# Mixture-of-experts phases of a four-layer block: shared down products in float32r, rest terms and sums on GpSimd, turned rows stored by ScalarE

## The reference, cut to what matters

```
x = x + ffn(layernorm(x))                       # before and after attention
logits = einsum('th,eh->te', x, gate_w)         # E = 8 experts, top K = 2
probs = softmax(logits); topk_w, topk_i = top_k(probs, 2); topk_w /= sum(topk_w)
g = einsum('th,ehi->eti', x, w_gate); u = einsum('th,ehi->eti', x, w_up)      # I = 352
eo = einsum('eti,eih->eth', silu(g) * u, w_down)
out = einsum('te,eth->th', combine, eo)
so = silu(x @ sw_gate) * (x @ sw_up) @ sw_down  # the shared expert, all tokens
out = out + sigmoid(x @ shared_gate_w) * so
```

## Time and profile before

| | us |
|---|---|
| median of the runs | 1923.58 |
| profiled execution, own time | 1933.64 |
| its span | 1931.9 |
| TensorE busy | 1852.8 (96%) |
| VectorE busy | 1354.6 (70%) |
| ScalarE busy | 1173.1 (61%) |
| GpSimd busy | 432.4 (22%) |
| first MoE phase, about | 212 to 635 |
| second MoE phase, about | 1510 to 1932 |
| one shared step with a piece of one-hots (steps 11 to 18 on TensorE) | 4.35 |
| VectorE: `hidden_rest` (L658), `source_rest` (L483), mean | 0.56, 0.42 |
| VectorE: the three operations of a one-hot piece (L615, L617, L620) | 0.75, 1.22, 0.75 |
| ScalarE: cast of 704 weight columns (L338) | 0.79 |

### The profile page before, as it was taken

How to read it: one execution, slowest core, us unless ns; L and a number is a source line. 1 busy time by engine, 2 the same in 40 slices (tenths; PEclk the granted TensorE clock), 3 DMA queues, 4 the chain that set the end, 5 groups by cost and what they waited for, 6 DMA issues and landing times. The chain is left out here.

```text
span 1931.9 us, 51788 instructions
## 1 busy us (share of the span) xinstructions
PE 1852.8 (96%) x19838; PEld 1431.7 (74%) x19838; DVE 1354.6 (70%) x2718; ACT 1173.1 (61%) x2355; POOL 432.4 (22%) x509
## 2 busy tenths in 40 slices
PE   7999899999999887999999999999999999999997
PEld 5788789999999644555555555565546789999997
DVE  7566678444436777899999999999944877444445
ACT  4222544444445543898899989989895644445443
POOL 4122001555542322000000000000000002555541
PEclk9999999999999999999999999999999999999999
DMA  7000211222226565321212111111005311222228
GB/s 306 1 1 1 79 45 35 72 77 78 76 68 200 140 171 144 80 52 47 52 47 47 41 42 42 41 42 42 3 3 200 103 36 35 77 75 78 76 68 267
DMA packets 86539, 149.13 MB, mean 77 GB/s; under 512 B 35620, under 2 KB 69284, under 8 KB 80612
## 3 DMA queue, kind: packets, MB, share of 16 engines
q1 hardware_dynamic: 68428, 103.24, 17.8%
q0 software_dynamic: 17856, 42.60, 8.0%
q10 hardware_dynamic: 24, 0.02, 0.0%
HBM read 96.68 MB, written 48.76 MB: 75 GB/s over the span
## 5 line engine op out<-in xcount | busy, mean ns | idle before, releaser
L2212 ACT ACTIVATE att_scores_pt<-att_scores_psE 128x512 f32<-128x512 f32 x1024 | 598.0, 597 | 69.0 <-PE att_scores_psE L1716 26.9
L1731 DVE TENSOR_REDUCE att_mx<-att_scores_psS 128x1 f32<-128x1024 f32 x472 | 577.9, 1224 | 50.1 <-PE att_scores_psS L1716 18.9
L1716 PE MATMUL att_scores_psE<-att_qs,att_ks 99*32 99x512 bf16 x4096 | 437.3, 382 | 4.0 <-DVE att_scores_psO L2242 3.2
L2314 PE MATMUL att_scores_psO<-att_scores_pt,att_va 128*17 128x256 f32 x4096 | 330.4, 379 | 2.9 <-ACT att_scores_osb L2217 1.3
L1716 PE MATMUL att_scores_psS<-att_ks,att_qs 96*32 96x512 bf16 x3776 | 308.4, 380 | 0.1
L1716 PEld LDWEIGHTS att_scores_psE<-att_qs,att_ks 99*32 99x32 bf16 x4096 | 136.0, 95 | 104.0 <-ACT att_scores_pt L2212 8.5
L658 DVE TENSOR_TENSOR moe_hidT_rest<-moe_ps,moe_hidT_high 128x384 fp32r<-128x384 f32 x142 | 79.1, 557 | 184.5 <-ACT moe_hidT_high L377 167.6
L2314 PEld LDWEIGHTS att_scores_psO<-att_scores_pt,att_va 128*17 128x17 f32 x4096 | 131.5, 98 | 103.3 <-issue 13.2
L865 PE MATMUL moe_ps<-W_rest,moe_srcT_high 128*128 (+2 forms) x824 | 200.6, 325 | 0.0
L283 POOL DMA_INDIRECT expert_rows<-work,moe_slots_i x142 | 140.0, 986 | 218.7 <-ACT work L399 101.3
L1716 PEld LDWEIGHTS att_scores_psS<-att_ks,att_qs 96*32 96x32 bf16 x3776 | 126.0, 97 | 78.1 <-issue 1.6
(11 more groups left out here) (325 smaller groups left out, 3154.0 us busy)
## 6 DMA issues: line engine op xcount, KB each, us to landing
W_gate_up<-in_gate_up_dram SPq DMA_DIRECT2D x2, 6346.0 KB, 22.3
work<-expert_rows SPq DMA_DIRECT2D x12, 1024.0 KB, 7.6
query_key_parts<-att_qkv_parts SPq DMA_DIRECT2D x64, 192.0 KB, 3.0
normalised_rows<-work SPq DMA_DIRECT2D x64, 128.0 KB, 1.9
att_qs<-query_key_parts SPq DMA_DIRECT2D x16, 384.0 KB, 4.4
att_ks<-query_key_parts SPq DMA_DIRECT2D x16, 384.0 KB, 4.5
W_down<-in_down_a_dram SPq DMA_DIRECT2D x2, 2304.0 KB, 28.0
work<-normalised_rows SPq DMA_DIRECT2D x36, 128.0 KB, 2.1
```

The costliest lines, as they stand in the source:

```text
L1716: last = nc.tensor.matmul(out[j:j + 32, :], stationary[:, j:j + 32], moving, start=True, stop=True, tile_position=(0, j), skip_group_check ...
L1731: return nc.vector.tensor_reduce(a.mx[g % 2][:, v:v + 1], bank[:, :, :].rearrange("p h k -> p (h k)"), AX.X, ALU.max)
L2212: nc.scalar.activation(pt[s % 2][:, r, :], psE[use % E_BANKS][:, :], ACT.Exp, scale=HD ** -0.5).then_inc(p_ready, 1)
L2314: last = nc.tensor.matmul(psO[32 * r:32 * r + VC, cols], va[g][:, kt, r * VC:(r + 1) * VC], pt[s % 2][:, r, cols], start=(kt == 0 and part ...
```

## The change

- **Down products.** In shared and late steps `down` makes the 9 float32r matmuls that routed steps make. A new `shared_down_high` holds the high part of the shared down weights (ScalarE, at the end of look step 0), its rest is made by GpSimd. ScalarE copies the hidden rows into the single `hidT_high` in every step, and VectorE makes `hidT_rest` in every step (`hidden_rest`).
- **Turned rows.** The look steps have the transposed rows of tiles 4 to 31 in `extra_T` already. ScalarE's queue stores them to a new DRAM tensor `turned_rows` (`store_turned`, 28 DMAs per phase); SyncE loads those of tiles 4 to 21 back already turned. For these 18 tiles TensorE's two transposes go, ScalarE casts the loaded tile, and GpSimd makes its rest (`loaded_rest`). `extra_T` has 7 buffers in place of 2.
- **GpSimd** makes the 16 rests of the routed gate and up weights, half of the 12 rests of the routed down weights, the 18 rests of loaded rows, one multiplication of each of the eight one-hot pieces (`tile_marks`), and the first of `combine`'s two sums (`pair`). VectorE loses these.

The core of the diff (waits, GpSimd's new functions and their order, ScalarE's stores, the callers on VectorE and TensorE):

```diff
 
+        turned = lambda n: not LOOK <= n < NA
+        turns = lambda n: n + 1 if n < LOOK else n + 1 - (NA - LOOK)
+        rest_made = lambda n: (srcT_split, turns(n)) if turned(n) else (loaded_split, n - LOOK + 1)
...
-        SPLIT_REST = {FOUND - 1: range(0, 1), FOUND: range(1, 3), FOUND + 1: range(3, 6), FOUND + 2: range(6, 9),
-                      FOUND + 3: range(9, 12)}
+        SPLIT_REST = {FOUND + 2: range(4, 7), FOUND + 3: range(7, 10)}
+        SPLIT_REST_POOL = {TABLES + 1: range(0, 1), TABLES + 2: range(1, 2), TABLES + 3: range(2, 3), TABLES + 4: range(3, 4), NA: range(10, 12)}
...
+            def load_turned(n):
+                x = n - LOOK
+                sp.wait_ge(T_stored[x % BESIDE], 16 * (x // BESIDE + 1))
+                sp.dma_start(src[ring(n)][:, 0:D], xt_d[:, x, :]).then_inc(early_loaded[ring(n) - 2], 16)
...
-            for n in range(LOOK, NA):
-                x = n - LOOK
-                sp.wait_ge(x_stored[x % BESIDE], 16 * (x // BESIDE + 1))
-                if n >= LOOK + SRC - 2:
-                    sp.wait_ge(T_done, n - (SRC - 2) + 1)
-                sp.dma_start(src[ring(n)][:, 0:D], kept[:, n, 0:D]).then_inc(early_loaded[ring(n) - 2], 16)
+                if n == 2:
+                    for first in range(LOOK, LOOK + SRC - 2):
+                        load_turned(first)
+            for n in range(LOOK + SRC - 2, NA):
+                sp.wait_ge(*rest_made(n - (SRC - 2)))
+                load_turned(n)
...
-            pool.wait_ge(hot_ready, 1)
-            nc.gpsimd.memset(cw[:, :, :], 0.0).then_inc(cw_zero, 1)
...
+            def shared_down_rest():
+                pool.wait_ge(shared_down, 1)
+                nc.gpsimd.tensor_tensor(W["down_rest"][:, :, SHARED, :], W["down"][:, :, SHARED, :], shared_down_high[:, :, :],
+                                        ALU.subtract).then_inc(shared_down_split, 1)
...
+            def loaded_rest(n):
+
+                pool.wait_ge(srcT_ready, n + 1)
+                nc.gpsimd.tensor_tensor(srcT_rest[0].rearrange("p k t -> p (k t)"), buffer(n)[:, 0:D],
+                                        srcT_high[0].rearrange("p k t -> p (k t)"), ALU.subtract).then_inc(loaded_split, 1)
...
+            def tile_marks(i):
+
+                pool.wait_ge(hot_ready, i + 1)
...
+                nc.gpsimd.tensor_tensor(hot_id[i % 2][:, :, 0, :], hot_j[:, :, :],
+                                        tile1[:, i * PIECE:(i + 1) * PIECE, None].to_broadcast([P, PIECE, NBT]), ALU.mult).then_inc(tiles_marked, 1)
...
+            def downs_rest(some):
...
+                    raw, high, rest = down_piece(i)
+                    pool.wait_ge(down_high, i + 1)
+                    nc.gpsimd.tensor_tensor(rest, raw, high, ALU.subtract).then_inc(early_down_rest, 1)
...
+            for i in range(5):
+                weights_rest(i)
+            shared_down_rest()
+            for i in range(5, KD * E):
+                weights_rest(i)
+            for n in range(LOOK, FOUND + 2):
+                loaded_rest(n)
+                i = n - 2 - TABLES
+                if 0 <= i < CH // PIECE:
+                    tile_marks(i)
+                if i == 0:
+                    nc.gpsimd.memset(cw[:, :, :], 0.0).then_inc(cw_zero, 1)
+                if n - 2 in SPLIT_REST_POOL:
+                    downs_rest(SPLIT_REST_POOL[n - 2])
...
-            for j in range(AHEAD):
+            for j in range(2):
                 fetch(j)
+            for n in range(FOUND + 2, NA):
+                loaded_rest(n)
+            for j in range(2, AHEAD):
+                fetch(j)
+            downs_rest(SPLIT_REST_POOL[NA])
...
+            def pair(q):
+
+                at = got[q % GOT]
+                pool.wait_ge(got_loaded[q % GOT], 16 * (q // GOT + 1))
+                nc.gpsimd.tensor_tensor(at[:, :, 0, :], at[:, :, 0, :], at[:, :, 1, :], ALU.add).then_inc(paired, 1)
+
+            for q in range(3):
+                pair(q)
             for g in BY_DMA:
                 pool.wait_ge(added[g], 16)
                 add_rows(g, 1)
+            for q in range(3, len(BY_DVE)):
+                pair(q)
...
-                nc.scalar.copy(extra_T[x % 2][:, :, :].rearrange("p k t -> p (k t)"), psX[x % BESIDE % 2][:, 0:D]).then_inc(x_srcT, 1)
+                if x >= BESIDE:
+                    act.wait_ge(T_stored[x % BESIDE], 16 * (x // BESIDE))
+                nc.scalar.copy(extra_T[x % BESIDE][:, :, :].rearrange("p k t -> p (k t)"), psX[x % BESIDE % 2][:, 0:D]).then_inc(x_srcT, 1)
+
+            def store_turned(x):
+                act.wait_ge(x_srcT, x + 1)
+                nc.scalar.dma_start(xt_d[:, x, :], extra_T[x % BESIDE].rearrange("p k t -> p (k t)")).then_inc(T_stored[x % BESIDE], 16)
...
 
             def source_out(n, u):
 
-                act.wait_ge(T_done, n + 1)
-                nc.scalar.copy(srcT_high[u].rearrange("p k t -> p (k t)"), psT[:, 0:D]).then_inc(srcT_ready, 1)
+                high = srcT_high[u].rearrange("p k t -> p (k t)")
+                if turned(n):
+                    act.wait_ge(T_done, turns(n))
+                    nc.scalar.copy(high, psT[:, 0:D]).then_inc(srcT_ready, 1)
+                    return
+                act.wait_ge(early_loaded[ring(n) - 2], 16 * ((n - LOOK) // (SRC - 2) + 1))
+                act.wait_ge(u_done, n)
+                nc.scalar.copy(high, buffer(n)[:, 0:D]).then_inc(srcT_ready, 1)
+
+            def shared_down_split_high():
+                nc.scalar.copy(shared_down_high[:, :, :], W["down"][:, :, SHARED, :]).then_inc(shared_down, 1)
...
+                if 0 < here <= LOOK:
+                    for i in range(BESIDE - 2, BESIDE):
+                        store_turned((n - 1) * BESIDE + i)
...
                     for i in range(2, BESIDE):
+                        store_turned(n * BESIDE + i - 2)
...
+                    if n == 0:
+                        shared_down_split_high()
...
             def source_rest(n, u):
+                if not turned(n):
+                    return
...
             def choose_second():
+                for u in range(BESIDE):
+                    dve.wait_ge(T_stored[u], 16 * (EX // BESIDE))
...
-                    dve.wait_ge(inv_ready, i)
+                    dve.wait_ge(tiles_marked, i)
...
                 nc.vector.tensor_tensor(hot_p[i % 2][:, :, :], iota_p[:, None, :].to_broadcast([P, PIECE, P]),
-                                        over(pos_p, P), ALU.is_equal)
-                dve.wait_ge(hot_ready, i + 1)
-                nc.vector.tensor_tensor(hot_id[i % 2][:, :, 0, :], hot_j[:, :, :], over(tile1, NBT), ALU.mult).then_inc(inv_ready, 1)
+                                        over(pos_p, P), ALU.is_equal).then_inc(inv_ready, 1)
...
                 at, t = got[q % GOT], BY_DVE[q] * GS
-                dve.wait_ge(got_loaded[q % GOT], 16 * (q // GOT + 1))
-                nc.vector.tensor_tensor(at[:, :, 0, :], at[:, :, 0, :], at[:, :, 1, :], ALU.add)
-                dve.drain()
+                dve.wait_ge(paired, q + 1)
                 dve.wait_ge(d_used, shared_added)
                 nc.vector.tensor_tensor(X[:, t:t + GS, :], X[:, t:t + GS, :], at[:, :, 0, :], ALU.add).then_inc(by_dve, 1)
...
-                if k == "routed":
-                    hidden_rest(n)
+                hidden_rest(n)
...
                 if rows_rest and half == 0:
-                    pe.wait_ge(srcT_split, n + 1)
+                    pe.wait_ge(*rest_made(n))
...
+                if n == 0:
+                    pe.wait_ge(shared_down, 1)
+                    pe.wait_ge(shared_down_split, 1)
+                shared = isinstance(e, int) and e == SHARED
+                for stationary, rests in ((hidT_high, False), (hidT_high, True), (hidT_rest, False)):
+                    if stationary is hidT_rest:
+                        pe.wait_ge(hidT_split, n + 1)
+                    for k in (range(KI - 1, -1, -1) if stationary is hidT_rest else range(KI)):
+                        if rests:
+                            weights = W["down_rest"][:, k, e, :]
+                        else:
+                            weights = shared_down_high[:, k, :] if shared else D_high[k][:, e, :]
+                        last = nc.tensor.matmul(psD[:, 0:D], stationary[:, k, :], weights, start=(stationary is hidT_high and not rests and k == 0),
+                                                stop=(stationary is hidT_rest and k == 0))
...
-                if here + 1 < NS:
+                if here + 1 < NS and turned(here + 1):
```

114 lines of the change are left out of this document (50 added, 64 removed).

## The result

The changed kernel takes 1954.23 us (median of 4 executions, 1951.18 to 1957.67) against 1923.99 us for the kernel before beside it: ratio 1.0161, 95% interval 1.0138 to 1.0183. The forecast was 1931.8.

The account below looks back on a forecast made before the run. TensorE, busy 96% of the span, was taken as the bound. Two phases of 0 - 5.4 + 5.5 = +0.1, plus +7.5 and +0.5 for late steps, gave +8.2: 1931.8 us, own range 1926 to 1938, wider range 1918 to 1943.

Parts of the forecast that it names:

- GpSimd's rests, "cost nothing": Sixteen gate-up rests and one shared down rest on GpSimd, 22 us, beside ScalarE's casts and needed only later: cost nothing.
- The rival with that mechanism: GpSimd and VectorE slow each other in steps 11 to 14: 1939 us with half the 1.8 us loss per step; chance 0.14.
- The line of 1.21 ns a column: GpSimd two-input operations: 1.21 ns a column above 0.42 us, giving 1.66 us for a 1024-column sum.
- The rule weighed in the prediction: Skill's GpSimd rate, about 2.6 cycles an element: 2.25 us for the 1024-column sum, whole sum about 0.6 us higher.
- Down products and transposes: Shared steps: float32r down products save 0.21 us a step, dropped transposes 0.13; shared steps from 9 on at 3.43 us.
- Steps 4 to 21 without the stop: Shared steps 4 to 21: -5.4 us per phase, from -6.1 with less gain in table steps 4 to 8.
- Look steps: Steps 0 to 3: products -0.6, transposes -0.1, add_shared waits -1.1, ScalarE's cast +0.8, 28 stores +1.0; sum 0.
- Tiles 20 and 21: Their rests wait behind slots and two gathers on GpSimd: TensorE stops 4.5 us per phase, clock fall +1.0; together +5.5.
- 323.4: Time in us at which TensorE wants tile 20's rest, after down, hidden transposes and a third of a gate-up.
- the first gather starts at 324.5: GpSimd's first gather, at 324.84 us before, starts 0.35 earlier when VectorE loses source_rest there.
- Late steps: VectorE waits 2.5 us for GpSimd's first sum, 7.5 for the fourth behind an accumulating DMA: +7.5 first phase, +0.5 second.
- Adding to the median: Difference worked out in the profiled execution (1933.64 us), then added to the median of 1923.58 us.

Follow-up runs that it names:

- m1: Short program replacing the kernel: six VectorE forms alone, then beside four GpSimd 704-column sums; six 512-column SBUF sums took 3.70 us alone, 9.58 beside.
- e1: Changed kernel with both sums of every combine on VectorE again, as before the change; ratio 1.0112 to the kernel before.
- e7: Changed kernel with combine sums, rests of tiles 20 and 21, marks and down rests on VectorE, shared down cast one place later; ratio 1.0014 to the kernel before.
- e16: Kernel before with shared down products in float32r alone, hidden_rest on VectorE every step, shared down cast after tile 1's copy, its rest on GpSimd; ratio 1.0015.
- e3: Changed kernel with the rests of loaded tiles 20 and 21 on VectorE instead of GpSimd; ratio 1.0116 to the kernel before.
- e11: Changed kernel with first sums still on GpSimd, but in turn with VectorE's, the first ahead of the accumulating DMAs; late steps 45.9 and 40.7 us.
- e10: Changed kernel keeping only float32r down products and turned rows; weight, row and down rests, marks and sums on VectorE, cast one place later; ratio 1.0019.
- e13: Changed kernel, unchanged, timed and profiled again; ratio 1.0156 to the kernel before.
- e15: Kernel before with each of the 28 look-step rows stored a second time by SyncE, to a place nothing reads; ratio 1.0019.

## Why the prediction was wrong

- **GpSimd's rests, "cost nothing": this step failed.** The text asked when a result is needed, and not what VectorE runs beside GpSimd. The rival with that mechanism had 0.14 and was priced in four steps per phase alone, at 7 us. In its place the runs showed VectorE and GpSimd holding each other (m1) in every stage that got work on GpSimd: VectorE's normalising operations at 811 ns for 413, GpSimd's three operations of a table step at 4.64 us for the 2.9 forecast, a wait of 1.8 us in step 22, and the sum of 5.64 us for 1.22 in the late steps. Taken off GpSimd, the sums give back 12.3 us (e1), and marks and down rests bring steps 12 to 17 from 26.5 to 23.8 us in each phase (e7). The Trainium skill, SBUF — State Buffer, section "Who interferes with whom", says which forms: VectorE's tensor_scalar in its two-port mode, and its instructions with two SBUF inputs against a GpSimd instruction that reads SBUF, while reductions and one PSUM operand are free. By that rule the six forms of m1 come out as measured. The prediction had cited only the short line of the Trainium skill's GPSIMD Engine Reference, "1. Specifications", which speaks of contention.
- **Durations of GpSimd.** The line of 1.21 ns a column gave 1.66 us for 1024 columns; 2.34 measured. The rule weighed in the prediction said 2.25, and was nearly right. The line went through two operations of different kinds, and the time depends on the kind: 704 columns took 1.67 us in m1 and 1.43, alone, as a weight rest in the changed kernel.
- **Down products and transposes.** Forecast 3.43 us for a shared step, 3.34 to 3.36 measured in steps 4 and 5. e16 has 3.56 for 3.78 to 3.80 in step 5, so the products are worth 0.22 to 0.24, where 0.21 was forecast; the transposes 0.2, not 0.13.
- **Steps 4 to 21 without the stop, -5.4 forecast.** Before the stop (steps 4 to 17) -0.4 and -0.1 came. With GpSimd's marks and down rests away e7 has -3.9 and -3.7 there: they ate it.
- **Look steps, 0 forecast, +4.6 and +5.7 measured.** The delay in step 0 has the forecast size (+0.8; gate and up of step 1 begin at 226.82 for 226.09), but two causes, the cast and the held normalising operations. The stores were right at nearly nothing on ScalarE (0.33 us each on its queue, beside its casts), although was misread: 0.32 us is the shortest of SyncE's stores, their median 0.44. Missing was that the clock then stayed at 0.50 for up to 15 us. What makes that long stays open: the stage grew with the float32r products alone as well (e16), and the changed kernel itself took 36.2 us in one phase and 41.3 in another.
- **Tiles 20 and 21, +4.5 and +1.0.** Right in mechanism and nearly in size: 4.2 us and a fall of the clock; e3 gives back 6.7 and 4.7 over steps 18 to 24. (The text's 323.4 should be 323.5 by its own terms.) The sentence that the first gather starts at 324.5 was off by 3.9 (328.44), because the look stage was longer and the steps behind it had hardly shrunk; TensorE came later by as much, so the stop kept its size.
- **Late steps, +7.5 and +0.5.** The size in the first phase was near (+10.1), for another cause, and that was luck. The sum behind tile 24's add waited 4.6 us for 2.5, and then was held for 4.4 more. The forecast cause is real (e11) but covered. In the second phase 8.7 us were lost and 5.6 covered by the end's DMAs: +3.1.
- **Adding to the median.** The irregular routed steps are in the profiled execution of the kernel before and not in that of the changed one; adding a difference to the median was right, since they don't belong to either kernel.
- **The whole.** By the table, the +8.2 forecast stands against +38: look stage +10.3 for 0, steps 4 to 21 +10.0 for +0.2, steps 22 to 24 +4.7 for 0, late steps +13.2 for +8.0.

## What to carry to other kernels

Before work is moved from VectorE to GpSimd, list in the same stretch GpSimd's two-input operations and VectorE's two-input or tensor_scalar operations that work in SBUF alone: their times nearly add up (m1), and in no stage here did moving work on top of that gain anything. Reductions, and sums with an operand in PSUM, ran free of it. Give GpSimd such work only where VectorE's neighbours read PSUM (the rests of loaded rows in e7, 0.75 us each: with them on VectorE, in e10, steps 4 to 17 took 1.9 and 2.3 us more). When one edit undone changes nothing, undo two together before clearing either: causes cover each other.

## What the runs showed of the hardware that was not expected

- A held VectorE instruction waited for both queued GpSimd sums, not for one: 5.64 us in place of 1.22 (in m1 the engines alternated, 2.15 us an operation). A held operation shows as a longer record without idle time before it, so the waits do not list it.
- In the look stage the clock stayed at 0.50 for 3 to 15 us behind much the same waits. In e10 TensorE stood still for 0.97, 0.16 and 0.26 us in look step 0 and step 1 then took 13.2 us; in the kernel before it was 0.97, 0.16 and 0.33, and 9.9. In the changed kernel's second phase it was 0.75, 0.16 and 1.06 in one execution, and step 1 took 9.4 us; 0.74, 0.16 and 0.39 in another (e13), and 13.9. With more bytes (e15) and with the float32r products (e16) the stage was longer in one profile each. What sets the length is still open.
- Irregular routed steps (most some 0.6 us longer, and mostly one of 2.7 to 4 at step 79) come and go between series: steps 25 to 92 took 241.6 us in some and 246 to 250 in others, with the same kernel.
